# Softmax denominators of layer 0: two blocks of keys in four column bands, then one small product that adds and spreads them

## The reference, cut to what matters

```python
q = (lat @ Wq).reshape(b, n, HEADS, DHEAD).transpose(0, 2, 1, 3)
k, v = jnp.split(ctx @ Wkv, 2, axis=-1)
...
k = apply_rope(k, cos[None, None], sin[None, None])
attn = jnp.einsum('bhnd,bhsd->bhns', q, k) * scale
attn = jnp.clip(attn, -11.0, 11.0)
attn = jax.nn.softmax(attn, axis=-1)
out = jnp.einsum('bhns,bhsd->bhnd', attn, v)
out = out.transpose(0, 2, 1, 3).reshape(b, n, INNER)
return out @ Wo + bo
```

## Time and profile before

| what | value |
|---|---|
| median of 3 runs | 3720.78 us (3720.1 to 3721.49) |
| the profiled execution | 3726.95 us |
| its span, first to last instruction | 3725.1 us |
| layer 0's attention in it | about 90.7 to 616 us |
| PE busy over the span | 2808.6 us (75%) |
| DVE busy | 2231.3 us (60%) |
| ACT busy | 1432.7 us (38%) |
| mean granted clock of TensorE | 0.851 |

### The profile page before, as it was taken

One profiled execution on the slowest core, in us unless ns is written; L12 is line 12 of the kernel. 1 busy time (PEld: TensorE's weight loads), 2 busy tenths in 40 slices (PEclk: granted clock), 3 DMA queues, 4 the chain that ended last, 5 costly groups with the idle time before them and its releaser, 6 DMA issues. The chain is left out here.

```text
span 3725.1 us, 39786 instructions
## 1 busy us (share of the span) xinstructions
PE 2808.6 (75%) x12862; PEld 1808.0 (49%) x12862; DVE 2231.3 (60%) x4947; ACT 1432.7 (38%) x2218; POOL 329.6 (9%) x145
## 2 busy tenths in 40 slices
PE   2999998354566666667999966888587696699588
PEld 2444445132233333336888844554443685354377
DVE  4666764865777677624555544656564555676377
ACT  2444442212787787732222212222143222166221
POOL 0000000020000000001212202011100110200021
PEclk8999999676777777768999978998888797799799
DMA  1000000024001111001111010000331010522010
GB/s 58 14 8 13 13 8 13 23 74 134 1 23 23 23 24 28 1 10 66 36 48 51 25 48 1 1 0 0 100 75 36 32 45 17 176 69 52 19 46 29
DMA packets 53741, 136.62 MB, mean 37 GB/s; under 512 B 8793, under 2 KB 29281, under 8 KB 48993
## 3 DMA queue, kind: packets, MB, share of 16 engines
q1 hardware_dynamic: 53600, 135.01, 12.2%
HBM read 106.28 MB, written 28.31 MB: 36 GB/s over the span
## 5 line engine op out<-in xcount | busy, mean ns | idle before, releaser
L1675 PE MATMUL ps<-m1e_x_part_s,m1e_up_part_s 128*128 128x512 f32 x1296 | 298.0, 391 | 22.0 <-POOL m1e_up_part_s L1771 15.9
L1445 ACT ACTIVATE l1a_over_s<-l1a_sc_s,l1a_minus_step_s 128x1024 bf16<-128x1024 f32 x256 | 290.0, 1139 | 3.0 <-DVE l1a_minus_step_s L1319 1.7
L1675 PEld LDWEIGHTS ps<-m1e_x_part_s,m1e_up_part_s 128*128 128x128 f32 x1296 | 243.8, 189 | 74.2 <-issue 23.7
L1259 DVE MAX8 l1a_cand_s<-ps 128x8 f32<-128x128 f32 x1024 | 213.0, 281 | 72.0 <-PE ps L1154 68.8
L1187 PE MATMUL ps<-l1a_probs_s,l1h_v_s 128*32 128x256 f32 x1024 | 126.5, 584 | 158.0 <-ACT l1a_probs_s L1453 156.5
L1431 ACT ACTIVATE l1a_sc_s<-ps,l1a_minus_tau_s 128x1024 f32<-128x1024 f32 x128 | 142.0, 1112 | 155.9 <-DVE l1a_minus_tau_s L1288 67.3
L1718 ACT ACTIVATE m1e_act_out_s<-ps 128x512 f32<-128x512 f32 x108 | 64.6, 598 | 346.8 <-PE ps L1675 346.8
L538 DVE TENSOR_SCALAR l0a_probs_s<-l0a_probs_s 128x1024 f32<-128x1024 f32 x128 | 88.4, 691 | 150.3 <-ACT l0a_probs_s L605 149.9
L974 DVE TENSOR_REDUCE l3a_shift_s<-ps 128x1 f32<-128x1024 f32 x128 | 150.3, 1219 | 46.1 <-PE ps L891 46.1
L605 ACT ACTIVATE l0a_probs_s<-ps 128x1024 f32<-128x1024 f32 x128 | 131.1, 1024 | 104.5 <-PE ps L455 103.3
L1154 PE MATMUL ps<-l1h_ka_s,l1h_qa_s 128*128 128x512 f32 x256 | 132.7, 564 | 49.7 <-DVE l1a_cand_s L1259 45.2
(11 more groups left out here) (530 smaller groups left out, 5873.9 us busy)
## 6 DMA issues: line engine op xcount, KB each, us to landing
m1ew_up_s<-m_up SPq DMA_DIRECT2D x9, 1536.0 KB, 6.2
l1h_ka_s<-l_k_parts SPq DMA_DIRECT2D x16, 512.0 KB, 8.0
l3h_ka_s<-l_k_parts SPq DMA_DIRECT2D x16, 512.0 KB, 8.1
m1ew_down_s<-m_down SPq DMA_DIRECT2D x9, 768.0 KB, 4.2
l0a_w_s<-l_w SPq DMA_DIRECT2D x16, 384.0 KB, 2.9
m3ew_up_s<-m_up SPq DMA_DIRECT2D x6, 768.0 KB, 4.2
l1h_qa_s<-l_q_parts SPq DMA_DIRECT2D x16, 256.0 KB, 6.0
l_v_groups<-l1p_v_all_s SPq DMA_DIRECT2D x8, 512.0 KB, 2.9
```

Source lines behind the costliest of these rows:

```text
L1259: ins = nc.vector.max(cand[:, r, 8 * (c + j * 4):8 * (c + j * 4) + 8], ps[:, A0 + f % 2, c * P:(c + 1) * P])
L1445: nc.scalar.activation(over[:, done % 2, :], sc[:, r, :], ACT.Relu, bias=minus_step[:, r:r + 1], accum_out=total[:, i, r:r + 1]).then_inc( ...
L1675: ins = nc.tensor.matmul(ps[:, 2 * (u % 2) + way, :], up_parts[a][:, k, way, c, :], x_parts[b][:, k, half * BANK:(half + 1) * BANK], start ...
```

## The change

The product with v stays as it is. The product with ones is made only after odd blocks, for two blocks at once: four products of 32 columns, one for each block and head, side by side in four column bands of bank 7. Rows 0 to 31 of the bank then hold head 0 of the even blocks, rows 32 to 63 head 1 of the even blocks, and rows 64 to 127 the same for the odd blocks. ACT copies the bank to `den` as before. A new product with a constant matrix `pair_sum` (ones in rows 0 and 64 for the first 64 columns, in rows 32 and 96 for the others) adds the two halves and spreads the sum over the 64 rows of each head, into bank 7 again. ACT copies that to `spread_den`, and DVE takes the reciprocal of it. SLOTS becomes 8. The wait of value product 0 for the copies is split: block 0 waits for `o_raw`, block 1 for the second copy of the denominators.

```diff
+            pool.memset(pair_sum[:, :], 0.0).then_inc(filled, 1)
...
+            both = pair_sum[:, :].rearrange("p (h c) -> p h c", h=2)
+            for part in range(2):
+                pool.wait_ge(made, 4 + part)
+                pool.affine_select(out=both, in_=both, compare_op=ALU.not_equal, fill=1.0, base=-64 * part,
+                                   pattern=[[-32, 2], [0, 64]], channel_multiplier=1).then_inc(made, 1)
...
-    SLOTS = 4
+    SLOTS = 8
...
                 if t == 0:
                     pe.wait_ge(v_ready, 2 * n + 4)
                     pe.wait_ge(o_copied, n + 1)
-                    pe.wait_ge(den_copied, n + 1)
+                if t == 1:
+                    pe.wait_ge(den_copied, 2 * n + 1)
                 pe.wait_ge(clip_done, NC_ * n + t + 1 + SLOTS)
...
-                for h in range(2):
-                    ins = nc.tensor.matmul(ps[64 * h:64 * h + 64, 7, :], ones[:, 0:64],
-                                           probs[:, t % SLOTS, h * NQ:(h + 1) * NQ], start=(t == 0), stop=(t == NC_ - 1))
-                ins.then_inc(pv_done, 1)
+                if t % 2 == 1:
+                    for i in range(4):
+                        ins = nc.tensor.matmul(ps[32 * i:32 * i + 32, 7, :], ones[:, 0:32],
+                                               probs[:, (t - 1 + i // 2) % SLOTS, i % 2 * NQ:(i % 2 + 1) * NQ],
+                                               start=(t == 1), stop=(t == NC_ - 1))
+                    ins.then_inc(pv_done, 2)
+
+            def denominators(n):
+                pe.wait_ge(den_copied, 2 * n + 2)
+                nc.tensor.matmul(ps[:, 7, :], pair_sum[:, :], den[:, :], start=True, stop=True).then_inc(den_made, 1)
...
+                    if last is not None and t == 2:
+                        denominators(n - 1)
                 if after is None:
                     value_product(n, p, NC_ - 2)
                     value_product(n, p, NC_ - 1)
+                    denominators(n)
...
-                dve.wait_ge(den_copied, n + 2)
-                nc.vector.reciprocal(rden[:, :], den[:, :]).then_inc(rden_ready, 1)
+                dve.wait_ge(den_copied, 2 * n + 3)
+                nc.vector.reciprocal(rden[:, :], spread_den[:, :]).then_inc(rden_ready, 1)
...
+            def copy_denominators(n):
+                act.wait_ge(den_made, n + 1)
+                act.wait_ge(rden_ready, n)
+                nc.scalar.activation(spread_den[:, :], ps[:, 7, :], ACT.Copy).then_inc(den_copied, 1)
...
+                    if t == 2 and last is not None:
+                        copy_denominators(n - 1)
...
                 if after is None:
                     copy_output(n)
+                    copy_denominators(n)
```

More of the change, by code:

```diff
@@ L94, in link, with constants @@
         self.wait()
-def constants(nc, ident, ones, slot_pick, spread):
+def constants(nc, ident, ones, slot_pick, spread, pair_sum):
     with Stage(nc, "const") as s:
@@ L110, in _ @@
             pool.memset(spread_f32[:, :], 0.0).then_inc(filled, 1)
-            pool.wait_ge(filled, 4)
+            pool.memset(pair_sum[:, :], 0.0).then_inc(filled, 1)
+            pool.wait_ge(filled, 5)
             pool.affine_select(out=ident[:, :], in_=ident[:, :], compare_op=ALU.not_equal, fill=1.0, base=0,
@@ L123, in _ @@
                                    pattern=[[-4, 6], [-1, 4], [0, 32]], channel_multiplier=1).then_inc(made, 1)
+            both = pair_sum[:, :].rearrange("p (h c) -> p h c", h=2)
[3 more added lines that the diff above has]
+                                   pattern=[[-32, 2], [0, 64]], channel_multiplier=1).then_inc(made, 1)
         @block.vector
         def _(dve):
-            dve.wait_ge(made, 4)
+            dve.wait_ge(made, 6)
             nc.vector.tensor_copy(spread[:, :, :].rearrange("p i n -> p (i n)"), spread_f32[:, :]).then_inc(rounded, 1)
@@ L338, in _, with rope_attention @@
             dve.wait_ge(added, TQ)
-def rope_attention(nc, name, ps, ones, q_t, ctx_t, w_dram, cos_dram, sin_dram, o_all):
+def rope_attention(nc, name, ps, ones, pair_sum, q_t, ctx_t, w_dram, cos_dram, sin_dram, o_all):
     DH = 64
@@ L369, in rope_attention @@
         o_raw, rden = s.sb("o_raw", [P, NQ]), s.sb("rden", [P, NQ])
-        den = s.sb("den", [P, NQ])
+        den, spread_den = s.sb("den", [P, NQ]), s.sb("spread_den", [P, NQ])
         tables, negated = s.sem("tables"), s.sem("negated")
@@ L385, in rope_attention @@
         pv_done = s.sem("pv_done")
-        o_copied, den_copied = s.sem("o_copied"), s.sem("den_copied")
+        o_copied, den_copied, den_made = s.sem("o_copied"), s.sem("den_copied"), s.sem("den_made")
         rden_ready, o_done = s.sem("rden_ready"), s.sem("o_done")
@@ L462, in value_product @@
                     pe.wait_ge(o_copied, n + 1)
-                    pe.wait_ge(den_copied, n + 1)
+                if t == 1:
+                    pe.wait_ge(den_copied, 2 * n + 1)
                 pe.wait_ge(clip_done, NC_ * n + t + 1 + SLOTS)
                 for h in range(2):
-                    nc.tensor.matmul(ps[64 * h:64 * h + 64, 6, :], v[:, p, t, 64 * h:64 * h + 64],
+                    ins = nc.tensor.matmul(ps[64 * h:64 * h + 64, 6, :], v[:, p, t, 64 * h:64 * h + 64],
                                      probs[:, t % SLOTS, h * NQ:(h + 1) * NQ], start=(t == 0), stop=(t == NC_ - 1))
-                for h in range(2):
-                    ins = nc.tensor.matmul(ps[64 * h:64 * h + 64, 7, :], ones[:, 0:64],
-                                           probs[:, t % SLOTS, h * NQ:(h + 1) * NQ], start=(t == 0), stop=(t == NC_ - 1))
-                ins.then_inc(pv_done, 1)
+                if t % 2 == 1:
[7 more added lines that the diff above has]
+                nc.tensor.matmul(ps[:, 7, :], pair_sum[:, :], den[:, :], start=True, stop=True).then_inc(den_made, 1)
             def first():
@@ L2463, in build @@
         slot_pick, spread = sb("slot_pick", [P, 60]), sb("spread", [P, 6, P], F32R)
+        pair_sum = sb("pair_sum", [P, P])
         x = sb("x_rows", [P, TQ, D])
@@ L2468, in by_feature @@
             return A[name + "_f"]
-        constants(nc, ident, ones, slot_pick, spread)
+        constants(nc, ident, ones, slot_pick, spread, pair_sum)
         load_x(nc, A["x"], x)
@@ L2504, in build @@
                 o_all = sb("l0_o_all", [P, 8, NT], stack=l0)
-                rope_attention(nc, "l0a", ps, ones, q_t, c_t, A["l0_w"], A["l0_cos"], A["l0_sin"], o_all)
+                rope_attention(nc, "l0a", ps, ones, pair_sum, q_t, c_t, A["l0_w"], A["l0_cos"], A["l0_sin"], o_all)
                 project_out(nc, "l0o", ps, o_all, 8, A["l0_wo"], A["L0_xattn_bo"], x)
```

## The result

The changed kernel takes 3689.8 us (median of 4 runs) against 3721.1 before, a ratio of 0.9916 (95% interval 0.9898 to 0.9933). Forecast were 3694.5 in a range of 3684 to 3708. A second comparison (e10_changed_again: six runs of the changed kernel, ten of the one before) gave 0.9924 (0.9909 to 0.9938), a difference of 27 us where the first gave 31 and the forecast was 26.

A forecast was written before the change was run, and what follows sets the result against it. PE was taken to bound layer 0's attention. The terms -43.4 + 12.8 + 1.5 + 2.3 - 0.3 + 0.85 gave -26.3 us, so 3694.5 us, in a range of 3684 to 3708.

The forecast's parts named there:

- PE bounds the stage, and the four bands run side by side in 1.00 us: Layer 0's attention: PE is the limit, and eight 32-column records take 1.00 us, both sides of the width change included.
- The rival with the bands two at a time: Four bands run two at a time, 1.86 us instead of 1.00, costing 53.3 us, so 3747.8; chance 0.05.
- The width change: On PE, between products of different column width: 0.15 us for each change, 64 to 32 priced like 128 to 64.
- The rival in which it is free: Going from 64 to 32 columns costs PE nothing, so 3685.2 us; chance 0.09.
- 62 of 64 pairs: Pairs of blocks gain 0.70 us each, except two lost to a 1.4 us wait for clip 7: 43.4 us gained.
- 15 x 0.86 for the product with `pair_sum`: The new product before scores 3 of a group adds two PE records, 0.86 us each time: 12.8 us lost.
- The wait of value product 1, 0.10: PE waits 0.10 us a group at value product 1 for ACT's second copy: 1.5 us lost.
- The stage's end, 2.3: After the last group the new product and second copy delay the reciprocal: 2.3 us lost, bounds 2.0 and 2.7.
- The constants, 0.85: At the start POOL's extra matrix fill and two selections delay DVE's cast: 0.85 us lost.
- DVE and ACT keep up: In full groups clip 7 keeps 2.7 us free, so PE stays the bound; rival with DVE as bound, chance 0.03.
- A full group of 30.7 us, PE busy all of it: A full group shortens from 32.5 to 30.7 us, with PE busy throughout.
- PE's own work explains the period: Before the change, eight steps of 2.99 and five projection units of 1.71 make 32.5 us a group.

The follow-up runs named there:

- e10_changed_again: The changed kernel run once more with no edit; 3693.5 us, 0.9924 of the kernel before.
- e2_pairs_of_64: Kernel before plus the change's setup, denominators made after odd blocks for two blocks, but in 64-wide bands two at a time; 3726.3 us, 1.0004 of the kernel before.
- e4_fours: Changed kernel with the four-band products made after every fourth block, two of them behind each other; 3688.9 us, 0.9911 of the kernel before.
- e6_finish_7: Changed kernel with DVE's reciprocal and multiplication of the group before moved from step 6 to step 7, behind clip 7; 3690.0 us, 0.9922 of the kernel before.
- e3_no_spread: Changed kernel without the product with pair_sum and the second copy, so its output is not the reference's; 3679.3 us, 0.9875 of the kernel before.
- e1_setup_only: Kernel before with pair_sum, eight slots and the tile spread_den added, denominators made as before; 3725.7 us, 1.0006 of the kernel before.
- e5_release_later: Changed kernel with PE's weights-free signal given at the end of step 7 instead of behind projection unit 4; 3683.0 us, 0.9904 of the kernel before.
- e9_all_fours: Changed kernel with later weights-free signal, reciprocal behind clip 7, and products with v and four-band products made in fours; 3673.7 us, 0.9869 of the kernel before.

## Why the prediction was right, step by step

- **PE bounds the stage, and the four bands run side by side in 1.00 us.** Right: 1.00 measured, and e2_pairs_of_64 shows that it is the whole gain. The rival with the bands two at a time (1.86) is what 64-wide bands do (1.82).
- **The width change.** 1.01 for the product with v before the bands and after even blocks: both as forecast, from the nearest row. The price (0.15 on its own side) holds for 64 to 32 as well, by e4_fours. The rival in which it is free falls.
- **62 of 64 pairs.** The wait for clip 7 is 1.28 us, forecast were 1.4. The last group takes 34.06 us as against 34.05 before. e6_finish_7, without the wait, gets 0.5 back.
- **15 x 0.86 for the product with `pair_sum`.** 0.86 in the timeline, 0.87 in e3_no_spread, which takes out a wait for its copy too.
- **The wait of value product 1, 0.10.** Not there: 1.98 from the new product to it, where the prediction had 1.99 for PE by itself and 2.09 with the wait, and no idle time in the trace. ACT began its copy 0.04 after PE's record ended and not 0.10. The product follows the end of the copy by 0.22, against 0.26 in the earlier trace rows, so little or nothing was to spare.
- **In its place** 0.13 a group came at projection unit 4, which the prediction didn't have. It comes with the setup (e1_setup_only). So the full group moved by 1.83 where 1.84 was forecast, with two small terms wrong that cancel by luck.
- **The stage's end, 2.3.** Too much, and below its bounds of 2.0 to 2.7: from value product 7 to the reciprocal are 5.20 us now and 3.52 before, so 1.7. The way from the copy of `den` to the reciprocal grew by 1.8 instead of 2.0, and the copies behind value product 7 began 0.13 earlier after it (2.20 instead of 2.33), where 0.15 later and another 0.15 were counted.
- **The constants, 0.85.** 1.01 measured.
- **DVE and ACT keep up.** Right; no full group shows a wait for a clip.
- **A full group of 30.7 us, PE busy all of it.** It takes 31.21, and PE idles for 0.28 of it.

The stage's own balance is -27.1 us, and with the constants -26.1, where the sum said -26.3. That it fits so well is partly luck: the end was counted 0.6 too dear, unit 4 and the constants too cheap. The first scores start 1.97 us later than before, 1.01 of it by the constants; in e4_fours, with the same constants, they start only 0.20 later, so the rest is not the change's. The first median moved by 31, the second by 27; the additional microseconds of the first lie within its interval (25 to 38 us). One step was wrong without harm: "PE's own work explains the period". Eight steps and five units sum to 32.5, and the period is 33.04. Of the missing half microsecond about 0.4 was PE's wait behind unit 4 (2.20 us, against 1.81 at that place in e5_release_later). Taken seriously, it would have pointed before any run at the place where e5_release_later gains 8.5 us.

## What to carry to other kernels

Where PE bounds a stage and the columns of its products are few, count how many bands run at once: the same eight records took 1.82 us in pairs and 1.00 in fours. In this kernel each visit from 128-wide work to a narrower width and back cost PE about 0.15 us on the narrow side and 0.2 on the wide side, so products of one width belong together; that was worth nearly as much here (20.6 us) as the whole change (27.1), until another engine's turn came (e9_all_fours). And a sum of PE's work that falls short of the period by half a microsecond is a wait with a place, and worth finding.

## What the runs showed of the hardware

A wait of 2.43 us on PE in e4_fours was followed by a fall of the granted clock (1.00 before 575 us, 0.66 in the 5 us after it) and 1.4 us more for 16 records; a wait of 1.28 us in the changed kernel, in the same place, was followed by the usual 1.07 us for eight records. A semaphore wait of PE for its own last product cost 0.53 us each time (2.34 to 1.81), though the trace shows only 0.28 of it as idle. Eight records of 512 columns took 1.00 us in four bands of 32 columns and 1.82 in 64-wide bands, the change of width included.
